# Graph attention with layer norm: the end of a group of rows moves from ScalarE and VectorE to VectorE's reductions and GpSimd

## The reference

```python
Wh = (h @ W.T).reshape(n, K, OUT_DIM).transpose(1, 0, 2)
score_src = jnp.einsum('knd,kd->kn', Wh, a1)[:, :, None]
score_dst = jnp.einsum('knd,kd->kn', Wh, a2)[:, None, :]
e = jax.nn.leaky_relu(score_src + score_dst, 0.2)
e = jnp.where((adj == 0)[None, :, :], -jnp.inf, e)
alpha = jax.nn.softmax(e, axis=-1)
h_prime = jnp.einsum('kij,kjd->kid', alpha, Wh)
gat = h_prime.transpose(1, 0, 2).reshape(n, K * OUT_DIM)
out = _layernorm(x + gat, axis=-1)
```

## Time and profile before

| | us |
|---|---|
| runs shown: median (lowest to highest) | 1690.55 (1688.36 to 1693.2) |
| the profiled execution, its own time | 1688.86 |
| its span, first to last instruction | 1686.8 |
| its mean granted TensorE clock, as a share of 2.4 GHz | 0.962 |
| idle of PE in which it waited for nothing shown ("issue"), before L685 | 52.6, in 22 pieces |
| wait of POOL for `quad_past` | 110.2 |

### The profile page before, as it was taken

The page is one execution under the profiler, slowest core; times in us unless marked ns, Lnnn a source line. Parts: engine busy times, 40 slices in busy tenths (PEclk is TensorE's granted clock), DMA queues, the critical chain, the costliest instruction groups (busy, mean ns, idle before and its releaser), DMA issues.

```text
span 1686.8 us, 79434 instructions
## 1 busy us (share of the span) xinstructions
PE 1439.9 (85%) x35205; PEld 1412.5 (84%) x35205; DVE 1636.8 (97%) x1804; ACT 1529.5 (91%) x2556; POOL 1435.6 (85%) x1589
## 2 busy tenths in 40 slices
PE   6069988998888989888898988899888898988986
PEld 6069988998888888888898888898888888888886
DVE  7989999999999999999999999999999999999997
ACT  3699999989989999999989999998999999899994
POOL 1689989897988989898898988889899898989983
PEclk9589999999999999999999999999999999999998
DMA  6266657566565656657466564755557565555630
GB/s 204 75 177 200 202 163 220 175 199 185 162 207 174 197 179 192 203 172 215 157 201 186 189 193 164 215 177 194 174 177 217 169 221 175 192 179 177 193 123 21
DMA packets 161833, 303.31 MB, mean 180 GB/s; under 512 B 9528, under 2 KB 22200, under 8 KB 161464
## 3 DMA queue, kind: packets, MB, share of 16 engines
q1 hardware_dynamic: 161464, 298.03, 56.5%
HBM read 293.67 MB, written 4.33 MB: 177 GB/s over the span
## 4 chain that ended last, share of the span: by engine, by line
DVE 40%; issue 29%; PE 20%; POOL 9%; DVEq 1%; ACT 1%; DMA 0%; SPq 0%; POOLq 0%; ACTq 0%
PE bank L685 17%; DVE step L527 16%; DVE step L522 12%; POOL step L326 6%; DVE step L529 3%; POOL edge L293 2%; PE bank L672 2%; POOL rstd L297 1%; DVE bank L484 1%; DVE rest L539 1%; DVE stats L592 1%; DVE late L573 1%; DVE xr L588 1%; DVE xr L583 1%; DVE G L445 1%
## 5 line engine op out<-in xcount | busy, mean ns | idle before, releaser
L403 ACT ACTIVATE step<-s_all,sd 128x512 uint8<-128x512 f32 x2304 | 1423.2, 719 | 46.1 <-PE bank L685 45.9
L326 POOL TENSOR_SCALAR step<-s_all,sd 128x512 uint8<-128x512 f32 x1280 | 916.8, 734 | 110.8 <-DVEq L616 110.2
L685 PE MATMUL bank<-G,step 128*128 128x99 bf16 x16384 | 789.2, 209 | 132.1 <-DVE step L529 98.4
L685 PEld LDWEIGHTS bank<-G,step 128*128 128x128 fp8e4 x16384 | 750.7, 98 | 155.9 <-DVE step L529 121.3
L539 DVE SCALAR_TENSOR_TENSOR rest<-step,bank 128x2048 int32<-128x2048 int32 x256 | 585.6, 2288 | 10.1
L685 PE MATMUL bank<-F,rest 128*128 128x66 f16 x16384 | 558.2, 195 | 20.8 <-issue 20.7
L685 PEld LDWEIGHTS bank<-F,rest 128*128 128x128 fp8e4 x16384 | 538.5, 98 | 22.2 <-issue 22.2
L293 POOL TENSOR_SCALAR edge<-adj_t 128x2048 int8<-128x2048 int32 x256 | 484.2, 1891 | 82.9 <-PE bank L672 61.0
L527 DVE SCALAR_TENSOR_TENSOR step<-bank,step 128x1536 int32<-128x1536 int32 x256 | 447.7, 1749 | 5.8 <-ACT step L403 5.8
L522 DVE SCALAR_TENSOR_TENSOR step<-s_all,sd,bank 128x512 uint8<-128x512 f32 x512 | 358.9, 743 | 11.4 <-issue 6.1
L672 PE MATMUL bank<-identb,edge 128*128 128x128 bf16 x2048 | 158.7, 221 | 10.5 <-issue 8.1
(11 more groups left out here) (74 smaller groups left out, 320.0 us busy)
## 6 DMA issues: line engine op xcount, KB each, us to landing
adj_t<-in_adj SPq DMA_DIRECT2D x512, 512.0 KB, 4.9
s_all<-sT_scratch SPq DMA_DIRECT2D x16, 1024.0 KB, 10.2
adj_t<-in_x SPq DMA_DIRECT2D x16, 256.0 KB, 5.7
xr<-in_x SPq DMA_DIRECT2D x16, 256.0 KB, 5.6
out<-xr SPq DMA_DIRECT2D x16, 256.0 KB, 5.4
sT_scratch<-late SPq DMA_DIRECT2D x2, 64.0 KB, 1.9
step<-in_L_gnn_W SPq DMA_DIRECT2D x1, 64.0 KB
a_col<-in_L_gnn_a SPq DMA_DIRECT2D x2, 0.5 KB
```

Source lines behind the costliest of these rows:

```text
L326: last = nc.gpsimd.tensor_scalar(step_u8[:, k % NS, h, n // E, :, n % E], s_all[:, g % 2, h], STEEP, d_steep[:, q * IB + n, h:h + 1], ALU. ...
L403: last = nc.scalar.activation(step_u8[:, q % NS, h, b // E, :, b % E], s_all[:, n, h], ACT.Sigmoid, scale=STEEP, bias=d_steep[:, q * IB + ...
L685: last = nc.tensor.matmul(acc[k][:, col:col + width], matrix[:, h, n // E, b * P:(b + 1) * P, n % E], values[:, q * IB + n, h].rearrange(" ...
```

## The change

It does five things.

- DVE takes the sums out of PSUM itself. `take_sums` is now on DVE, in the first quad of the next group behind `step`: for each bank it waits for PE's close and runs two reductions, one over the three parts of `top`, one over the two of `low`. ACT's copies and DVE's three additions of parts are gone. PE's next group waits for `acc_taken` from DVE.
- Five instructions of the end of a group go to POOL (`close`, parts 0 to 4, behind its quads 2, 3, 4, 9 and 10). DVE keeps the reciprocal (quad 8), the statistics (quads 11 and 12) and the shift (quad 13). ACT normalises behind its quad 15 in place of 14.
- POOL no longer waits for `quad_past`.
- DVE's two comparisons of a quad move ahead: `compare` of quad q + 1 stands between `step` and `rest` of quad q. The smaller mask goes first, then the larger.
- The scores are loaded by head, 256 KB at a time, behind the edges of quads 6, 8, 10 and 12.

```diff
+        CLOSING = (2, 3, 4, 9, 10)
+        S_QUADS = (6, 8, 10, 12)
-        SCALED = 14
+        SCALED = 15
...
-            def load_s(g, n):
-                src = sT_v[g].unsqueeze(0).to_broadcast([P, HEADS, ROWS])
-                sync.dma_start(s_all[:, n], src).then_inc(s_loaded[n], 16)
+            def load_s(g, n, h):
+                src = sT_v[g, h:h + 1].unsqueeze(0).to_broadcast([P, 1, ROWS])
+                sync.dma_start(s_all[:, n, h:h + 1], src).then_inc(s_loaded[n], 16)
...
+            def close(g, part):
...
+                if part == 0:
+                    pool.wait_ge(acc_taken, done((g + 2) * BANKS))
+                    nc.gpsimd.tensor_tensor(low, low, per_row(beta[:, rows, :], HC), ALU.mult).then_inc(low_set, 1)
+                elif part == 1:
+                    nc.gpsimd.tensor_tensor(top, top, per_row(alpha[:, rows, :], HC), ALU.mult).then_inc(top_set, 1)
+                elif part == 2:
+                    pool.wait_ge(top_set, 2 * g + 1)
+                    pool.wait_ge(low_set, g + 1)
+                    nc.gpsimd.tensor_tensor(top, top, low, ALU.add).then_inc(top_set, 1)
+                elif part == 3:
+                    pool.wait_ge(rden_set, g + 1)
+                    pool.wait_ge(stored, 16 * done(g))
+                    nc.gpsimd.tensor_tensor(y.rearrange("p b (h c) -> p (b h) c", h=HEADS), top[:, :, 0:D_OUT],
+                                            per_row(rden[:, :, :], D_OUT), ALU.mult).then_inc(sum_set, 1)
+                else:
+                    pool.wait_ge(sum_set, 2 * g + 1)
+                    pool.wait_ge(res_loaded, 16 * g + 16)
+                    nc.gpsimd.tensor_tensor(y, y, res, ALU.add).then_inc(sum_set, 1)
...
-                    if k > 1:
-                        pool.wait_ge(quad_past, k - 1)
...
-                    if q == 11 and g > 0:
+                    if q in CLOSING and g > 0:
+                        close(g - 1, CLOSING.index(q))
+                    if q == 13 and g > 0:
                         inverse_deviation(g - 1)
...
-                    nc.scalar.copy(late[:, b * USED:b * USED + n_ch * CH], acc[b][:, 0:n_ch * CH]).then_inc(acc_act, 1)
...
+                for b, h in DVE_TILES:
+                    last = nc.vector.scalar_tensor_tensor(step_u8[:, q % NS, h, b // E, :, b % E], s_all[:, n, h],
+                                                          d_neg[:, q * IB + b, h:h + 1], edgeT8[q % 2][:, b // E, :, b % E],
+                                                          ALU.is_ge, ALU.logical_and)
+                last.then_inc(dve_compared, 1)
...
+            def take_sums(g):
+
+                for b in range(BANKS):
+                    n_ch = chunks_of(b)
+                    sums = acc[b][:, 0:n_ch * CH].rearrange("p (k c) -> p k c", c=CH)
+                    top, low = (t[:, b * PER_BANK:b * PER_BANK + n_ch] for t in (top_sums, low_sums))
+                    dve.wait_ge(acc_done, at(dve, g * BANKS + b + 1))
+                    for to, part in ((top, sums[:, :, 0:BC]), (low, sums[:, :, BC:CH])):
+                        last = nc.vector.tensor_reduce(to, part.rearrange("p k (s c) -> p k c s", c=HC), AX.X, ALU.add)
+                    last.then_inc(acc_taken, 1)
...
-                    take_step(g, q, n)
+                    take_step(g, q)
+                    if q == 0 and not first:
+                        take_sums(g - 1)
+                    if q + 1 < QUADS:
+                        compare(g, q + 1, n)
+                    elif not last:
+                        compare(g + 1, 0, 1 - n)
                     take_rest(g, q, waits=not first or q >= NL)
-                    if q > 0:
+                    if q >= 8:
                         next(closing, None)
-                    dve.sem_inc(quad_past, 1)
...
-                pe.wait_ge(acc_act, done(g * BANKS + k + 1))
+                pe.wait_ge(acc_taken, done(g * BANKS + k + 1))
```

More of the change, by code:

```diff
@@ L117, in gat_layernorm @@
         s_rows = late[:, NX * ROWS:NX * ROWS + 2 * P].rearrange("p (n r) -> p n r", n=2)
-        acc_sb = late[:, :].rearrange("p (k c) -> p k c", c=CH)
+        top_sums, low_sums = (late[:, n * CHUNKS * HC:(n + 1) * CHUNKS * HC].rearrange("p (k c) -> p k c", c=HC) for n in range(2))
         rden = sb("rden", [P, IB, HEADS], fp32)
@@ L255, in _ @@
                         sync.wait_ge(s_stored, 32)
-                        load_s(0, 0)
+                        for h in range(HEADS):
+                            load_s(0, 0, h)
                     if q == 4 and g > 0:
@@ L260, in _ @@
                         load_rows(g - 1)
-                    if q == 6 and g + 1 < GROUPS:
+                    if q in S_QUADS and g + 1 < GROUPS:
                         if g == 0:
@@ L293, in take_edges, with per_row @@
                 nc.gpsimd.tensor_scalar(edge[:, k % N8], adj_t[:, k % NA], 1.0, -1.0, ALU.min, ALU.max).then_inc(edge_set, 1)
+            def close(g, part):
+                top, low = top_sums, low_sums
+                def per_row(v, width):
+                    return v.rearrange("p b h -> p (b h)").unsqueeze(2).to_broadcast([P, CHUNKS, width])
+                rows = slice(g * IB, (g + 1) * IB)
+                if part == 0:
[16 more added lines that the diff above has]
+                    nc.gpsimd.tensor_tensor(y, y, res, ALU.add).then_inc(sum_set, 1)
             def inverse_deviation(g):
@@ L330, in _ @@
                         take_edges(k + N8)
-                    if q == 11 and g > 0:
+                    if q in CLOSING and g > 0:
+                        close(g - 1, CLOSING.index(q))
+                    if q == 13 and g > 0:
                         inverse_deviation(g - 1)
+            for part in range(len(CLOSING)):
+                close(GROUPS - 1, part)
             inverse_deviation(GROUPS - 1)
@@ L379, in _ @@
             second_part(UNITS - 1)
-            def take_sums(g):
-                act.wait_ge(var_set, done(g))
-                for b in range(BANKS):
-                    n_ch = chunks_of(b)
-                    act.wait_ge(acc_done, at(act, g * BANKS + b + 1))
-                    nc.scalar.copy(late[:, b * USED:b * USED + n_ch * CH], acc[b][:, 0:n_ch * CH]).then_inc(acc_act, 1)
             def normalise(g):
@@ L405, in group @@
                     last.then_inc(act_compared, 1)
-                    if q == 1 and not first:
-                        take_sums(g - 1)
                     if q == SCALED and not first:
@@ L553, in wait_last @@
                     dve.wait_ge(dve_chain, CHAIN0 + g * CHAIN_STEP + got[0])
-                rows = bass.ds(g * IB, IB)
-                def per_row(v, width):
-                    return v.rearrange("p b h -> p (b h)").unsqueeze(2).to_broadcast([P, CHUNKS, width])
-                top, low = acc_sb[:, :, 0:HC], acc_sb[:, :, BC:BC + HC]
-                dve.wait_ge(acc_act, done((g + 2) * BANKS))
-                nc.vector.tensor_tensor(low, low, acc_sb[:, :, BC + HC:CH], ALU.add)
-                then(nc.vector.tensor_tensor(top, top, acc_sb[:, :, HC:2 * HC], ALU.add))
-                yield
-                wait_last()
-                nc.vector.tensor_tensor(low, low, per_row(beta[:, rows, :], HC), ALU.mult)
-                then(nc.vector.tensor_tensor(top, top, acc_sb[:, :, 2 * HC:BC], ALU.add))
-                yield
-                wait_last()
-                then(nc.vector.tensor_tensor(top, top, per_row(alpha[:, rows, :], HC), ALU.mult))
-                yield
-                wait_last()
-                then(nc.vector.tensor_tensor(top, top, low, ALU.add))
-                yield
-                wait_last()
-                then(nc.vector.tensor_scalar(rden[:, :, :], top[:, :, D_OUT].rearrange("p (b h) -> p b h", h=HEADS),
+                dve.wait_ge(top_set, 2 * g + 2)
+                then(nc.vector.tensor_scalar(rden[:, :, :], top_sums[:, :, D_OUT].rearrange("p (b h) -> p b h", h=HEADS),
                                              TINY, None, ALU.max))
                 wait_last()
-                then(nc.vector.reciprocal(rden[:, :, :], rden[:, :, :]))
-                yield
-                wait_last()
-                dve.wait_ge(stored, 16 * done(g))
-                then(nc.vector.tensor_tensor(y.rearrange("p b (h c) -> p (b h) c", h=HEADS), top[:, :, 0:D_OUT],
-                                             per_row(rden[:, :, :], D_OUT), ALU.mult))
-                yield
-                wait_last()
-                dve.wait_ge(res_loaded, 16 * g + 16)
-                then(nc.vector.tensor_tensor(y, y, res, ALU.add))
-                yield
-                wait_last()
+                nc.vector.reciprocal(rden[:, :, :], rden[:, :, :]).then_inc(rden_set, 1)
+                for _ in range(3):
+                    yield
+                dve.wait_ge(sum_set, 2 * g + 2)
                 for b in range(IB):
@@ L601, in finish @@
                 nc.vector.tensor_scalar(mv[:, :, 1], mv[:, :, 1], EPS, None, ALU.add).then_inc(var_set, 1)
```

(5 more changed lines are left out.)

44 lines of the change are left out of this document (23 added, 21 removed).

## The result

The changed kernel takes **1639.0 us** (median of 4 runs, 1634.11 to 1642.13), beside 1689.45 for the kernel before: a ratio of 0.9695, 95% interval 0.9666 to 0.9725. Run again beside the experiments it took 1640.0, ratio 0.971 (0.9661 to 0.9758). The profiled execution took 1639.39 with a span of 1637.6.

The account below looks back on a forecast made before the run. DVE was taken as the bound at 99.3 us a group; 15 x (99.3 - 94.8 - 0.3 - 0.4) = 57 saved, with -1 and +2 a span of 1630.8, forecast 1635 us, range 1615 to 1670.

Parts of the forecast that it names:

- 6.1 us of tensor_tensor leave: DVE, end of a group: eight tensor_tensor instructions go, 6.76 us a group busy, 6.1 us of queue after overlaps.
- 0.12 us a quad from the order: DVE: comparisons between small mask and `rest` cut that mask's pitch from 0.45 to 0.33 us, saving 1.9 a group.
- 3.5 us of reductions: DVE, taking the sums: twelve reductions out of PSUM add 3.5 us a group, 4.5 at the upper end.
- 94.8 us a group with no waits: DVE's time for a group after the change: 99.3 - 6.1 - 1.9 + 3.5, if nobody makes DVE wait.
- the mean of 99.3: DVE's us a group in the kernel before, over 15 groups: sixteen quads 90.2, some 9 for the group's end.
- R: Moment DVE's reciprocal behind quad 8 is ready; POOL then needs 11.1 us, DVE wants it after 11.0: 0.3 wait.
- PE, 0.4 us a group: Group's start: PE idles 3 us for `rest`, perhaps at lower clock afterwards; DVE waits 0 to 1.2, taken as 0.4.
- a slack of 1.3 us: Time between PE's transposed edges being ready and DVE's comparison wanting them, after the new order; before it was 4.4.
- Group 0 and the tail, -1 and +2: Group 0: ACT's 5.54 replaces DVE's 5.64 a quad, -1 us; tail: later denominator and two more POOL instructions, +2.
- The loads at nothing, their return at +55: Scores in 256 KB pieces costed at nothing for PE; PE's dry stretch returning once a group: about 1690 or 1691.
- my rival of a dry stretch unhidden: PE feeds DVE too late: 4.7 us lost once a group, about 1691 (0.03); two losses a group, 1730 (0.07).
- The other rivals: POOL becomes the bound, 1656 us (0.09); reductions at twice the price, 1686 (0.08); scores by head change nothing, about 1690.

## Why the prediction was right

Forecast 1635, measured 1639, by the mechanism named. Step by step:

- **DVE is the bound.** Right: 97% busy, and its busy time and the span fell by 54 and 49 us.
- **6.1 us of tensor_tensor leave.** Right as a sum. Their length above 0.7 us I read as a fixed price; the run with loads by head shows that 12 us of it in all hung on PE's dry stretches.
- **0.12 us a quad from the order.** Right gross: 5.51 a quad, and the two runs with the old order show it once and twice. Net of what it causes it is 8 us in the changed kernel, 9 in the kernel before with the loads by head, and a loss of 7 in the kernel before as it was.
- **3.5 us of reductions.** 3.53. The price of 4.25 that the Trainium skill, VectorE: DVE Perf Modes, section The TRN2 errata, gave doesn't hold for the queue; it is nearer to the durations (0.452 and 0.348 for 0.43 and 0.33).
- **94.8 us a group with no waits.** 94.95 in a group that has 0.5 of waits, and 0.56 of the shift that no term held (below), so the queue is some 0.9 shorter than the sum. The sum began from the mean of 99.3, and that mean held 0.8 a group of idle time before L522 (11.4 us in all), of which the 6.1 us where DVE turns its loop are still there:

```profile
L522 DVE SCALAR_TENSOR_TENSOR step<-s_all,sd,bank 128x512 uint8<-128x512 f32 x512 | 358.9, 743 | 11.4 <-issue 6.1 <-DVE stats L592 3.4 <-PE bank L672 1.1
```

- **POOL.** 1.25 us for each of the five; measured 1.05 to 1.32, 5.8 a group for my 6.25. DVE waited for its comparisons of quad 11 as computed at R, but 0.16 us in nine groups, not 0.3 in each.
- **PE, 0.4 us a group.** Under-sized: 14.3 / 15 = 0.95. The cause named, the lower clock behind the idle time of 2.9 us, is right in part: it came in eight groups of fifteen, made DVE wait at once in three of them (3.3 us), and the run with `rest` behind the sums takes away some 8 of the 14 us. The other part are short gaps in PE's stream, up to 1.6 us each, later in the group. The prediction took them at nothing, because PE had been busy for 4.80 of 5 us in one stretch with a 256 KB load; against a slack of 1.3 us they weren't nothing.
- **Missed: the shift.** L620 has two SBUF inputs too, on 4 elements. It lasts 0.838 us for 0.275 before, 0.56 a group. I had said that DVE was left with no such instruction "of size"; for a wait its size is of no account.
- **Group 0 and the tail, -1 and +2.** The reductions of group 1 begin at 183.14, where the mask before ended at 183.70: -0.6. From the end of the last masks to the last instruction it is 20.7 us for 19.5: +1.2.
- **The loads at nothing, their return at +55.** The first held. The second, my rival of a dry stretch unhidden, was far too dear: with the single load back the changed kernel is 3 us slower. What neither had is that the loads by head would bring 15 us of their own in the kernel before.

The two terms that were too small, 0.55 and 0.56 a group, make 17 us. POOL (0.2) and the waits that went with the mean of 99.3 (0.3, behind the statistics and for PE) give back 7 to 8, and the span came out 6.8 us above the 1630.8 forecast; the last 2 us I can't place. So the closeness of the total is in part luck: two misses in one direction, and nearly half of them made good by terms that were too large. The other rivals didn't come about: POOL's wait stays at 1.4 us in all, the reductions cost their forecast.

## What to carry to other kernels

Put independent work between two instructions of one engine that wait for each other, but count what it takes from the slack of those who feed that engine; here 31 us gross were 8 net. Look at every group before you name a cause from one: the group shown first above had the slow clock, and seven of fifteen had the same idle time without it. When an engine's instructions are longer than their size explains, ask who shares its ports and what keeps the two in step: a stall on a third engine can lengthen them. A tiny instruction can be the dearest, if it must wait for a pause of another engine.

## What the hardware showed that was not expected

A DVE instruction with two SBUF inputs doesn't always get its turn at the next boundary of POOL's instructions: 0.92 us, up to the first boundary, in the changed kernel, but 8.87 us, past eleven boundaries, where POOL had work without a gap. The Trainium skill, SBUF — State Buffer, section SBUF: two separate sides, lets the one that starts first keep the port for that instruction, which covers the 0.92 but not the 8.87.

TensorE's granted clock fell behind an idle time of 2.88 us in some groups (0.57 in the five us around and behind the one at 858.9) and stayed at 1.00 behind the same idle time in others (at 477.1); behind 1.56 us or less in the same place it stayed up in all fifteen. What decides between the two cases is open.

PE stood idle with nothing shown for up to 5.4 us behind a 1 MB broadcast in the kernel before. The trace points to what it waited for: the DMA queue of kind "instruction" (q8, 276 packets of 16 KB) has a packet landing in each of the fourteen stretches of over 1.5 us, 1.2 to 1.6 us before the stretch ends, for instance from 493.15 to 494.12 in the one that ends at 495.40. With four loads of 256 KB the gaps are 2.1 us at most in any of these kernels; why they are only 2.6 and 2.7 us at most with the 1 MB in the changed kernel and in the one with `rest` behind the sums is open.
